# Router logits from the attention output product: a folded gate, and expert weights loaded in another order

## The chip, the cores and the metric

The kernel runs on one core of a Trainium2 chip. The metric is the device time of one execution in microseconds (us); lower is better. A core has five engines with an instruction stream each: TensorE (PE, with its weight loads as PEld), VectorE (DVE), ScalarE (ACT), GpSimd (POOL) and SyncE (SP), which here only issues DMAs. The engines are ordered by semaphores alone.

## The reference

One sequence of T = 1024 tokens of width D = 256 passes a mixer with a gated feed-forward part, a linear mixing layer, causal attention over 8 heads of 64, and a mixture of 8 experts of which each token takes two. Layer normalisations stand between. What the change touches is the seam of the last two:

```python
z = softmax(q k' / 8 + causal mask) v          # 8 heads of 64 columns
x3 = x2 + z @ wo                               # residual, [1024, 256]
h = (x3 - mean(x3)) / sqrt(var(x3) + 1e-5)
logits = h @ gate.T                            # [1024, 8]
top_v, top_i = top_k(softmax(logits), 2)
weights = top_v / sum(top_v)                   # per token
y = x3 + sum over the two: weight * (silu(h @ w1[e]) * (h @ w3[e])) @ w2[e]
```

## The kernel before, in words

The program is written by hand, engine by engine; the order of each stream is the order of the Python loops, and every dependency is a semaphore.

**q, k, v.** 24 blocks (`FILLS`), 12 for each half of the tokens: four of q, four of k, four of v, 512 columns each. TensorE makes a block as 6 products in fp32r (values split in a high and a low part, three part products over two halves of the width, lines 1618 and 1622) into PSUM banks 2 to 7 in turn; it waits only for the block six places back. ScalarE reads k blocks and even blocks, VectorE k blocks and odd blocks. Banks 0 and 1 hold transposed inputs, `hT`, which is the layer-normalised x2.

**Attention.** 8 tiles of 128 tokens (i), 4 pairs of heads each, so 32 steps m = 4i + rel and 6 more that empty the pipeline. In step m TensorE makes `scores(m)`, transposes the probabilities of the heads before (`probs_transposed`, line 1660), and multiplies them with v (`attended(m - 2)`, line 1675, two heads side by side in 64 columns of the array each). Between these, by rel: `reciprocals_transposed(i - 1)` at rel 2, `attention_out(i - 1)` at rel 3 (the product with wo, line 1694, 256 columns into bank 6 or 7). VectorE finds the row maxima before each exponential of ScalarE; at rel 3 it adds the product to x and takes mean and variance (`add_attention`, `route_variance`, to line 1250); GpSimd makes 1/sqrt from it.

**The router of tile t = i - 2** follows a step later. VectorE normalises (line 1254, rel 0), TensorE transposes the rows (1703), ScalarE copies them (803), TensorE multiplies them with the gate (1709, 8 columns), VectorE takes the maximum (1259), ScalarE the exponentials (808), VectorE chooses the two largest at rel 1 (`route_choice`, 1264 to 1272), TensorE counts with two products, a triangle of ones and a full one (`route_counts`, 1718 and 1719), and VectorE makes weights and slot numbers (`route_tail`, `route_slots`, to 1294). GpSimd then scatters each token's row to its two slots of `expert_in` (592). For the last tile all of this stands alone, with `keep_busy` products of no use between, which keep TensorE occupied.

**The seam.** After the last slots VectorE makes a table of expert tiles (1324 to 1341). SyncE loads the first two tiles of slots (436) once table and scatter are done. ScalarE and VectorE split the first expert's weights (849, 1364) when all up matrices are loaded and all of x is stored (`s_out`, line 873).

**Expert weights on SyncE's queue.** w1 and the first four w3 are loaded at the start of attention. Then SyncE stores tiles 0 to 6 of x, each when it is ready (lines 411 to 413), and only then loads w3 of experts 6 and 7, w2 of experts 0 to 4 (when all scores are done), w3 of 4 and 5 (when zT of the last tile is done), w2 of 5 to 7 and the last 64 rows of all w2 (`m_w2t`, a strip of 64 partitions), and stores the last tile of x (432). A w3 matrix is 704 KB, a w2 matrix 640 KB, the strip 512 KB.

**Experts.** 23 tiles of 128 slots. A tile: 2 transposes of its rows (1757), 6 transposes of the activation of the tile before (1777; 704 columns padded with zeros to 768), 18 products up in fp32r (1769), 6 products down in float32, which are 12 records (1789; the sixth has 64 rows of zeros, which lines 586 and 1383 write). TensorE's order in the steady loop:

```python
def body(i, b, first=False):
    pe.wait_ge(s_exT, i + 2)
    expert_x(i + 2, b)
    expert_aT(i, b)
    expert_up(i + 1, 1 - b)
    expert_down(i, b, first)
```

## Time and profile before

| | |
|---|---|
| median of 3 executions | 556.26 us (556.05 to 556.93) |
| the profiled execution | 554.53 us |
| its span, first to last instruction | 552.7 us |
| mean clock granted to TensorE | 0.98 of full speed |
| TensorE / VectorE / ScalarE / GpSimd busy | 508.2 / 356.0 / 278.5 / 184.6 us |
| share of the chain that ended last, TensorE | 76% |
| q, k, v: stretch of the span | 159 to 197 us |
| attention | 197 to 343 us |
| from the last scores' work to the first expert products | 343 to 374 us |
| experts | 374 to 546 us |
| ScalarE's copy of up to 512 columns (line 791), mean | 0.51 us |

The span is what the profiler sees between the first and the last instruction; the execution's own time lies 1.8 us above it. Busy time is no measure of a bound by itself: what an engine waited for, and whether anything waited for it, is in the chain and the waits. A record is one instruction in the trace; a float32 product is two of them.

### The profile page before, as it was taken

The numbers are of one execution on the slowest core, as the hardware profiler recorded it, in microseconds if no ns is written. First come the engines' busy times: TensorE is split into PE (matmuls) and PEld (weight loads), VectorE is DVE, ScalarE is ACT, GpSimd is POOL, SyncE is SP. The second block draws the span as 40 slices with busy tenths as digits, with TensorE's granted clock in tenths as the row PEclk, the third lists the DMA queues.
The fourth block names the chain that finished last, engine by engine and source line by source line (L and its number), as shares of the span: only waits on it lengthen the run. The fifth ranks groups of instructions, "written<-read, shape, count | busy, mean of one in ns | idle before, by whom it ended". The sixth has DMA issues, their size and how long they took to land.

```text
span 552.7 us, 9980 instructions
## 1 busy us (share of the span) xinstructions
PE 508.2 (92%) x3285; PEld 417.9 (76%) x3286; DVE 356.0 (64%) x875; ACT 278.5 (50%) x529; POOL 184.6 (33%) x236
## 2 busy tenths in 40 slices
PE   3988989998989998989999998797999999999994
PEld 1647978887968866667778786676888888888883
DVE  5884879547457335656668675456777777777761
ACT  2585554216123265656555563025666666666651
POOL 3026629984032032422223110310433333333332
PEclk9997999999999999999999999779999999999999
DMA  8999001000010069000000005861112222222211
GB/s 322 406 338 291 2 25 53 1 0 1 2 38 1 0 239 406 34 31 20 11 31 12 20 20 193 311 193 40 23 37 38 38 38 38 38 38 38 29 16 23
DMA packets 25813, 47.47 MB, mean 86 GB/s; under 512 B 2224, under 2 KB 21168, under 8 KB 25392
## 3 DMA queue, kind: packets, MB, share of 16 engines
q1 hardware_dynamic: 21408, 41.76, 21.4%
q0 software_dynamic: 4080, 5.15, 6.3%
q8 instruction: 22, 0.36, 0.3%
q10 hardware_dynamic: 288, 0.08, 0.1%
q14 instruction: 15, 0.12, 0.1%
HBM read 32.01 MB, written 14.98 MB: 85 GB/s over the span
## 4 chain that ended last, share of the span: by engine, by line
PE 76%; DVE 10%; ACT 5%; issue 5%; POOL 1%; DMA 1%; POOLq 0%; SPq 0%; ACTq 0%; DVEq 0%
PE ps L1769 16%; PE ps L1789 11%; PE ps L1562 8%; PE ps L1660 5%; PE ps L1645 4%; PE ps L1675 4%; PE ps L1618 4%; PE ps L1584 4%; PE ps L1777 3%; PE ps L1457 2%; PE ps L1694 2%; PE ps L1622 2%; DVE early L1012 2%; PE ps L1544 1%; ACT work L783 1%
## 5 line engine op out<-in xcount | busy, mean ns | idle before, releaser
L1769 PE MATMUL ps<-split,xsT 128*128 128x512 f32 (+1 forms) x414 | 93.7, 379 | 1.1 <-DVE split L1364 1.0
L1769 PEld LDWEIGHTS ps<-split,xsT 128*128 128x128 f32 x414 | 74.7, 188 | 13.4 <-issue 1.2
L1364 DVE TENSOR_TENSOR split<-early,split 128x1408 fp32r<-128x1408 f32 x46 | 72.8, 1622 | 6.4 <-ACT split L849 6.0
L1789 PE MATMUL ps<-mid,work 128*128 x276 | 63.4, 379 | 0.8 <-ACT work L838 0.8
L849 ACT CAST split<-early 128x1408 fp32r x46 | 62.6, 1365 | 1.1 <-issue 1.1
L615 POOL TENSOR_TENSOR rstd<-mhalf 128x1 f32<-128x1 f32 x23 | 21.7, 942 | 118.7 <-ACT work L845 118.7
L1214 DVE TENSOR_REDUCE nmax<-ps 128x1 f32<-128x128 f32 (+7 forms) x64 | 45.4, 751 | 21.9 <-PE ps L1645 21.7
L1789 PEld LDWEIGHTS ps<-mid,work 128*128 128x128 f32 x276 | 52.0, 190 | 7.0 <-issue 1.0
L1346 DVE TENSOR_TENSOR work<-work,ps 128x704 f32<-128x704 f32 x23 | 20.4, 888 | 42.4 <-PE ps L1769 42.4
L834 ACT ACTIVATE work<-ps 128x704 f32<-128x704 f32 x22 | 16.8, 762 | 48.4 <-PE ps L1769 48.4
L783 ACT ACTIVATE work<-ps,nmax 128x128 f32<-128x128 f32 (+7 forms) x48 | 35.9, 751 | 2.9 <-DVE nmax L1214 2.9
L616 POOL DMA_INDIRECT out<-work,slot_i x23 | 35.8, 1558 | 4.1 <-issue 2.1
L1660 PE MATMUL ps<-cst,work 128*128 128x128 f32 x216 | 31.4, 278 | 1.8 <-DVE work L1220 1.0
L791 ACT COPY work<-ps 128x512 f32<-128x512 f32 (+3 forms) x32 | 16.2, 506 | 32.8 <-PE ps L1660 32.2
L592 POOL DMA_INDIRECT expert_in<-rows,slot_i x16 | 16.3, 1019 | 47.6 <-DVE slot_i L1294 45.1
L1660 PEld LDWEIGHTS ps<-cst,work 128*128 128x128 f32 x216 | 24.2, 141 | 7.1 <-ACT work L783 4.9
L756 ACT ACTIVATE work<-ps 128x512 f32<-128x512 f32 x16 | 9.6, 598 | 34.6 <-PE ps L1562 34.6
L1457 PE MATMUL ps<-rows,early 128*128 128x512 f32 x48 | 23.5, 638 | 1.5 <-ACT rows L645 1.5
L569 POOL CAST q_hi<-mid 128x128 fp32r<-128x128 f32 x32 | 10.0, 311 | 41.7 <-PE ps L1645 41.1
L598 POOL TENSOR_TENSOR rstd<-veps,mhalf 128x1 f32<-128x1 f32 x8 | 4.5, 567 | 56.6 <-DVE veps L1250 56.6
L791 ACT COPY rows<-ps 128x512 f32<-128x512 f32 (+3 forms) x32 | 16.3, 508 | 12.1 <-PE ps L1660 11.6
L1675 PE MATMUL ps<-work,mid 128*64 128x128 f32 x288 | 19.3, 278 | 2.8 <-ACT early L797 2.7
(259 smaller groups left out, 1144.0 us busy)
## 6 DMA issues: line engine op xcount, KB each, us to landing
early<-m_w SPq DMA_DIRECT2D x16, 704.0 KB, 9.1
expert_in<-pad SPq DMA_DIRECT2D x8, 1040.0 KB, 12.3
mid<-m_w SPq DMA_DIRECT2D x8, 640.0 KB, 8.9
work<-expert_in SPq DMA_DIRECT2D x23, 130.0 KB, 2.8
early<-factors SPq DMA_DIRECT2D x1, 2048.0 KB, 11.5
early<-wq SPq DMA_DIRECT2D x1, 2048.0 KB, 15.5
mid<-f_w SPq DMA_DIRECT2D x1, 2048.0 KB, 19.8
rows<-x_in SPq DMA_DIRECT2D x4, 256.0 KB, 3.9
```

Source lines behind the costliest of these rows:

```text
L616: nc.gpsimd.indirect_dma_start(out=out, out_offset=bass.IndirectOffsetOnAxis(ap=dest_now[:, b:b + 1], axis=0), in_=ey[:, b], in_offset=Non ...
L783: nc.scalar.activation(probs[u % 4][:, 0:w], score_row(u), ACT.Exp, bias=nmax[:, u:u + 1], accum_out=psums[:, u:u + 1]).then_inc(s_pr, 1)
L791: nc.scalar.copy(pT[u % 4][:, 0:w], ps[:, pT_banks(u), 0:w]).then_inc(s_pT, 1)
L849: nc.scalar.copy(split_w[0][:, :, w * I:(w + 1) * I], expert_w(e, w)).then_inc(s_whi[w], 1)
L1214: V.tensor_reduce(nmax[:, u:u + 1], score_row(u), AX_X, ALU.max, negate=True).then_inc(s_max, 1)
L1364: V.tensor_tensor(lo, expert_w(e, w), hi.bitcast(F32), ALU.subtract).then_inc(s_wlo[w], 1)
L1457: last = mm(ps[:, 2 + q % 4, :], win_sb[:, k, fb * P:(fb + 1) * P], hT[:, k, g * GW:(g + 1) * GW], start=(k == 0), stop=(k == KD - 1))
L1562: last = mm(ps[:, 2 + 2 * w + q % 2, :], fw13_split[pw][:, w * KD + k, f * P:(f + 1) * P], hT_split[ph][:, k, g * GW:(g + 1) * GW], start= ...
L1660: last = nc.tensor.transpose(ps[:, pT_banks(u) + j // 4, (j % 4) * P:(j % 4 + 1) * P], probs[u % 4][:, j * P:(j + 1) * P], ident)
L1675: last = mm(ps[h * DH:(h + 1) * DH, 6 + i % 2, pair * P:(pair + 1) * P], v_sb[:, j, n * DH:(n + 1) * DH], pT[(2 * m + h) % 4][:, j * P:(j ...
L1769: last = mm(up_flat[:, c0:c1], xsT[px][b][:, k, :], split_w[pw][:, k, c0:c1], start=(k == 0 and px == pw), stop=(k == KD - 1 and px == 1))
L1789: last = mm(ps[:, 6, 0:D], eaT[:, b, c, :], we[:, c, :], start=(c == 0), stop=(c == IB - 1))
```

## The change

The gate (256 x 8) is centred: the mean of each column is subtracted, so that logits of x3 need no subtraction of the row's mean. With a centred gate g, the logits before the factor 1/sqrt(var) are x2 @ g + z @ (wo @ g). `wo @ g` is computed once and put beside wo as 8 more columns (`wo_m`, 264 wide), so that the output product makes it along; x2 @ g is computed from `hT` with the gate as the stationary operand (8 columns), turned to tokens by small products, and multiplied by sqrt(var(x2)) (`base_logit`). The choice is made from these sums right behind the variance; the two weights come from the exponential of the difference of the two largest. Transposes, copy, product with the gate and maximum of the router are gone. The expert loads are interleaved, the last store of x goes to ScalarE's queue, and the last of six transposes and products of an expert tile are cut to the 64 columns and rows that hold data, without the zeros.

```diff
@@ SyncE: loads behind the stores of tiles 0 to 6
-            for e in range(below_k, E):
+            def load_w3(e):
                 pairs_over = -(-(E * KD * I + (e + 1) * KD * I - K_AT) // T)
                 sp.wait_ge(s_sc, (TT - 1) * HEADS + 2 * min(pairs_over, PAIRS))
                 sp.dma_start(ew3[:, e], m_w3[:, e]).then_inc(s_e13, 16)
-            sp.wait_ge(s_sc, TT * HEADS)
+            def load_w2(e):
+                pairs_over = max(0, -(-((e + 1) * IB * D - QB * T) // T))
+                if pairs_over:
+                    sp.wait_ge(s_sc, (TT - 1) * HEADS + 2 * min(pairs_over, PAIRS))
+                sp.dma_start(ew2[:, e, 0:(IB - 1) * D], m_w2[:, e]).then_inc(s_e2, 16)
             below_v = 2 * QB * T // (IB * D)
-            for e in range(below_v):
-                sp.dma_start(ew2[:, e, 0:(IB - 1) * D], m_w2[:, e]).then_inc(s_e2, 16)
+            sp.wait_ge(s_qs, STEPS)
+            for e in range(2):
+                load_w2(e)
+            load_w2(2)
+            load_w3(below_k)
+            load_w2(3)
+            load_w3(below_k + 1)
+            load_w2(4)
             sp.wait_ge(s_zT, TT)
...
-            sp.wait_ge(s_x3, TT)
-            sp.dma_start(out[(TT - 1) * P:T, :], x[:, TT - 1, :]).then_inc(s_out, 16)
@@ GpSimd
-                if i == TT + 1:
-                    pool.wait_ge(s_pv, TT * HEADS // 2)
-                    nc.gpsimd.memset(mid[ILAST:P, :]...., 0.0).then_inc(s_w2pad, 1)
@@ ScalarE
             for q in range(FILLS):
+                if q in (16, 18):
+                    h = (q - 16) // 2
+                    act.wait_ge(s_woTp, h + 1)
+                    nc.scalar.copy(base_T[:, h * GW:(h + 1) * GW], ps[0:E, 1, :])
+                    nc.scalar.copy(woT[:, h, :], ps[:, 0, :]).then_inc(s_woT, 1)
...
-            def routed_feature_major(i):
...
             def logits_exp(i):
-                act.wait_ge(s_lmax, i + 1)
-                nc.scalar.activation(prob_e[:, i, :], ps[:, 6 + i % 2, D:D + E], ACT.Exp, ...)
+                act.wait_ge(s_ldiff, i + 1)
+                nc.scalar.activation(prob_e[:, i, 0:TOP], prob_e[:, i, 0:TOP], ACT.Exp).then_inc(s_lexp, 1)
...
+            act.wait_ge(s_x3, TT)
+            act.dma_start(out[(TT - 1) * P:T, :], x[:, TT - 1, :]).then_inc(s_out, 16)
             act.wait_ge(s_eid, 1)
             act.wait_ge(s_e13, 2 * E * 16)
             act.wait_ge(s_out, (TT + 1) * 16)
@@ VectorE
+            def centre_gate():              # at q == 14
+                dve.wait_ge(s_gsum, 1)
+                link(V.scalar_tensor_tensor(gate_sb, ps[:, 0, 0:E]..., -1.0 / D, gate_sb, ALU.mult, ALU.add))
+                link(V.tensor_copy(gate_r[:, 0], gate_sb))
+                V.tensor_tensor(gate_r[:, 1], gate_sb, gate_r[:, 0].bitcast(F32), ALU.subtract).then_inc(s_gc, 1)
+            def read_gate_fold():           # at q == FILLS - 2
+                link(V.tensor_tensor(spread, veps[:, :], rstd[:, :], ALU.mult))
+                dve.wait_ge(s_fold, 1)
+                V.tensor_copy(wo_m[:, :, D:], ps[:, 1, 0:QB * E]...)
+                V.tensor_tensor(base_logit, ps[:, 1, QB * E:QB * E + TT * E]..., spread..., ALU.mult).then_inc(s_folded, 1)
...
-            def route_max(t):
...
             def route_choice(t):
-                dve.wait_ge(s_lexp, t + 1)
-                link(V.reciprocal(rs[2][:, t:t + 1], rs[1][:, t:t + 1]))
-                link(V.tensor_scalar(prob_e[:, t, :], prob_e[:, t, :], rs[2][:, t:t + 1], None, ALU.mult))
-                link(V.max(top_v[:, t, :], prob_e[:, t, :]))
+                link(V.tensor_tensor(rank_e[:, t, :], ps[:, at, D:D + E], base_logit[:, t, :], ALU.add))
+                link(V.max(top_v[:, t, :], rank_e[:, t, :]))
...
+            def route_difference(t):        # two copies as in route_tail, then
+                V.tensor_scalar(prob_e[:, t, 0:TOP], top_v[:, t, 0:TOP], top_v[:, t, 0:1], rstd[:, t:t + 1],
+                                ALU.subtract, ALU.mult).then_inc(s_ldiff, 1)
+            def route_weights(t):           # waits for s_lexp; sum, reciprocal, product; increments s_slots
...
                 if rel == 3 and 1 <= i <= TT:
                     add_attention(i - 1)
                     route_variance(i - 1)
+                    route_choice(i - 1)
                 if rel == 0 and i >= 2:
-                    route_max(i - 2)
+                    route_normalise(i - 2)
+                    route_difference(i - 2)
+                    route_slots(i - 2)
                 if rel == 1 and i >= 2:
-                    route_tail(i - 2)
-                    route_slots(i - 2)
+                    route_weights(i - 2)
@@ TensorE
+            def gate_sums():                # before block 13
+                pe.wait_ge(s_gate, 32)
+                for k in range(KD):
+                    last = mm(ps[:, 0, 0:E], ones, gate_sb[:, k, :], start=(k == 0), stop=(k == KD - 1))
+                last.then_inc(s_gsum, 1)
+            def fold_inputs(h):             # before blocks 15 and 17; waits for s_wo, s_gc, s_woT
+                for part, (pw, ph) in enumerate(W_PARTS):
+                    for k in range(KD):
+                        mm(ps[0:E, 1, :], gate_r[:, pw, k, :], hT_split[ph][:, k, h * GW:(h + 1) * GW], ...)
+                for c in range(QB):
+                    last = nc.tensor.transpose(ps[:, 0, c * P:(c + 1) * P], wo_m[:, c, h * P:(h + 1) * P], ident)
+                last.then_inc(s_woTp, 1)
+            def gate_folded():              # before block 20; waits for s_woT
+                for c in range(QB):
+                    for k in range(KD):
+                        mm(ps[:, 1, c * E:(c + 1) * E], woT[:, k, c * P:(c + 1) * P], gate_sb[:, k, :], ...)
+                for t in range(TT):
+                    last = mm(ps[:, 1, (QB + t) * E:(QB + t + 1) * E], base_T[:, t * P:(t + 1) * P], ident[0:E, 0:E], ...)
+                last.then_inc(s_fold, 1)
...
             def scores(m):
+                if m == 0:
+                    pe.wait_ge(s_folded, 1)
...
-                    last = mm(ps[:, 6 + i % 2, 0:D], zT[:, c, :], wo_sb[:, c, :], ...)
+                    last = mm(ps[:, 6 + i % 2, 0:D + E], zT[:, c, :], wo_m[:, c, :], ...)
...
-            def route_transposed(i):        # keep_busy(16, 0) for the last tile
...
-            def route_logits(i):
...
             def route_counts(i):
                 if i == TT - 1:
-                    keep_busy(14, 0)
+                    keep_busy(20, 0)
...
-                if rel == 0 and i >= 2:
-                    route_transposed(i - 2)
...
-                if rel == 1 and i >= 2:
+                if rel == 0 and i >= 2:
                     route_counts(i - 2)
                 if 2 <= m <= STEPS + 1:
                     attended(m - 2)
-                if rel == 0 and i >= 2:
-                    route_logits(i - 2)
...
             def expert_x(i, b):
                 if isinstance(i, int) and i == 0:
-                    keep_busy(24, 0)
+                    keep_busy(16, 0)
...
             def expert_aT(i, b):
...
-                    last = nc.tensor.transpose(ps[:, 4 + c // 4, (c % 4) * P:(c % 4 + 1) * P],
-                                               ea[:, b, c * P:(c + 1) * P], ident)
+                    w = P if c < IB - 1 else ILAST
+                    last = nc.tensor.transpose(ps[0:w, 4 + c // 4, (c % 4) * P:(c % 4 + 1) * P],
+                                               ea[:, b, c * P:c * P + w], ident)
...
             def expert_down(i, b, first=False):
...
-                    last = mm(ps[:, 6, 0:D], eaT[:, b, c, :], we[:, c, :], ...)
+                    w = P if c < IB - 1 else ILAST
+                    last = mm(ps[:, 6, 0:D], eaT[0:w, b, c, :], we[0:w, c, :], ...)
...
+            keep_busy(56, 0)
             pe.wait_ge(s_e13, 2 * E * 16)
-            keep_busy(40, 0)
```

## Rows read from the trace of the kernel before

**Rows 1.** Stretches: busy us of PE, PEld, DVE, ACT, POOL; clock; DMA share; GB/s.

```profile
159.00:197.00 38.00, 37.47 (x171) 30.19 (x168) 17.38 (x36) 12.15 (x21) 6.43 (x13) 1.00 0.00 0
197.00:343.40 146.40, 137.45 (x1347) 108.60 (x1345) 95.50 (x270) 85.89 (x219) 37.32 (x75) 1.00 0.24 90
343.40:374.50 31.10, 24.86 (x169) 20.33 (x168) 14.78 (x63) 4.88 (x10) 6.37 (x6) 0.78 0.71 256
```

**Rows 2.** The chain that ended last: start us, us, what; blocks and one expert tile.

```profile
180.32 11.15 PE ps L1618 x48
...
527.14 0.66 PE ps L1777 x6
527.80 3.81 PE ps L1769 x18
531.61 2.59 PE ps L1789 x12
```

**Rows 3.** Timeline of the tail: start us, us, engine, line, operation, idle before.

```profile
341.47 1.97 PE L1675 MATMUL ps<-work,mid 128*64 128x128 f32 x32
...
347.13 3.68 PE L1675 MATMUL ps<-rows,mid 128*64 128x128 f32 x32
...
356.42 0.15 DVE L1250 TENSOR_SCALAR veps<-mv 128x1 f32<-128x1 f32 x1
...
357.27 1.97 DVE L1254 TENSOR_SCALAR rows<-rows,mv,rstd 128x256 f32<-128x256 f32 x1 [0.69 <-POOL rstd L598]
357.29 1.80 POOL L586 MEMSET mid<- 64x2048 f32 x1
...
365.67 0.17 DVE L1294 CAST slot_i<-rs 128x2 uint32<-128x2 f32 x1
...
368.95 0.18 DVE L1341 TENSOR_SCALAR region<-bias_sb 128x24 int32<-128x24 f32 x1
```

**Rows 4.** The chain in the tail: last scatter and first tile's load.

```profile
367.46 2.44 DMA expert_in<-rows,slot_i
...
370.94 2.00 DMA work<-expert_in
```

**Rows 5.** Timeline of TensorE, 312 to 319 us, at changes of the array's form.

```profile
313.32 0.73 PE L1645 MATMUL ps<-k_hi,q_hi 64*128 64x512 f32 x4
...
314.91 0.44 PE L1703 MATMUL ps<-cst,rows 128*128 128x128 f32 x2
315.19 0.93 PE L1660 MATMUL ps<-cst,rows 128*128 128x128 f32 x7
316.05 1.75 PE L1675 MATMUL ps<-work,mid 128*64 128x128 f32 x28
317.73 0.61 PE L1709 MATMUL ps<-gate_sb,rows 128*128 128x8 f32 x4
318.19 1.07 PE L1660 MATMUL ps<-cst,work 128*128 128x128 f32 x8
```

**Rows 6.** Waits of TensorE, 197 to 262 us: total, times, longest.

```profile
PE ps L1718 <- DVE rt L1272: 1.6, 2, 1.0
...
PE ps L1703 <- DVE rows L1254: 0.6, 1, 0.6
```

**Rows 7.** Timeline of SyncE's queue in the tail.

```profile
337.28 0.33 SPq L413 DMA_DIRECT2D out<-rows  x1
...
353.23 0.81 SPq L425 DMA_DIRECT2D early<-m_w  x2
```

**Rows 8.** Stretches of the tail, columns as in rows 1.

```profile
347.00:351.00 4.00, 4.00 (x34) 3.65 (x35) 0.75 (x5) 0.00 (x0) 1.81 (x2) 0.50 1.02 415
351.00:354.00 3.00, 2.95 (x15) 2.22 (x15) 0.69 (x1) 0.59 (x1) 0.18 (x1) 0.72 0.16 58
357.00:359.00 2.00, 0.00 (x0) 0.00 (x0) 1.73 (x1) 0.00 (x0) 1.94 (x2) 1.00 1.01 418
363.00:366.00 3.00, 3.00 (x17) 2.39 (x15) 1.84 (x15) 0.00 (x0) 0.00 (x0) 0.50 1.07 214
```

More of the change, by code:

```diff
@@ L207, in build @@
         base_e = view(dts_t, 0, TT + 1, E)
-        rs_t = sb("rs", 12 * TT)
-        rs = [rs_t[:, i * TT:(i + 1) * TT] for i in range(12)]
-        top_f = view(rs_t, 8 * TT, TT, TOP)
-        slot_f = view(rs_t, 10 * TT, TT, TOP)
+        rs_t = sb("rs", 8 * TT)
+        rs = {n: rs_t[:, i * TT:(i + 1) * TT] for i, n in ((1, 3), (2, 4), (4, 8), (5, 9))}
+        top_f = view(rs_t, 4 * TT, TT, TOP)
+        slot_f = view(rs_t, 6 * TT, TT, TOP)
         top_i_t = sb("top_i", TT * 8, U32); top_i = view(top_i_t, 0, TT, 8)
@@ L219, in build @@
         w_first, w_second = bias_sb[:, 0:24], bias_sb[:, 24:48]
+        base_logit = view(bias_sb, 0, TT, E)
+        spread = rs_t[:, 0:TT]
         dest_now = slot_i_t[:, 0:2]
@@ L282, in build @@
         s_zT, s_ao, s_x3 = sem("zT"), sem("attn_out"), sem("x3")
-        s_rT, s_rTc, s_lg, s_lmax, s_lexp, s_chosen, s_cnt = (sem(n) for n in (
-            "routed_transposed", "routed_T", "logits", "logit_max", "logit_exp", "chosen", "counts"))
+        s_ldiff, s_lexp, s_chosen, s_cnt = (sem(n) for n in (
+            "logit_difference", "logit_exp", "chosen", "counts"))
+        s_gsum, s_gc, s_woTp, s_woT, s_fold, s_folded = (sem(n) for n in (
+            "gate_summed", "gate_centred", "wo_transposed", "wo_T", "gate_folded", "gate_fold_read"))
         s_slots, s_scat, s_table, s_dest = sem("slots"), sem("scattered"), sem("tile_table"), sem("destinations")
@@ L1589, in _ @@
             transposes(PH_ATT, 0)
+            def gate_sums():
[4 more added lines that the diff above has]
+            def fold_inputs(h):
+                pe.wait_ge(s_wo, 16)
+                pe.wait_ge(s_gc, 1)
+                if h:
+                    pe.wait_ge(s_woT, h)
+                for part, (pw, ph) in enumerate(W_PARTS):
+                    for k in range(KD):
+                        mm(ps[0:E, 1, :], gate_r[:, pw, k, :], hT_split[ph][:, k, h * GW:(h + 1) * GW],
+                           start=(part == 0 and k == 0), stop=(part == 2 and k == KD - 1))
+                for c in range(QB):
+                    last = nc.tensor.transpose(ps[:, 0, c * P:(c + 1) * P], wo_m[:, c, h * P:(h + 1) * P], ident)
+                last.then_inc(s_woTp, 1)
+            def gate_folded():
+                pe.wait_ge(s_woT, 2)
+                for c in range(QB):
+                    for k in range(KD):
+                        mm(ps[:, 1, c * E:(c + 1) * E], woT[:, k, c * P:(c + 1) * P], gate_sb[:, k, :],
+                           start=(k == 0), stop=(k == KD - 1))
+                for t in range(TT):
+                    last = mm(ps[:, 1, (QB + t) * E:(QB + t + 1) * E], base_T[:, t * P:(t + 1) * P], ident[0:E, 0:E],
+                              start=True, stop=True)
+                last.then_inc(s_fold, 1)
             pe.wait_ge(s_pwlo, 3)
@@ L1740, in _ @@
                     probs_transposed(2 * m - 1)
-                if rel == 1 and i >= 2:
+                if rel == 0 and i >= 2:
                     route_counts(i - 2)
```

83 lines of the change are left out of this document (35 added, 48 removed).

## The prediction, made before the changed kernel was seen

> **What bounds the kernel now.** I read the page's slices first, then a table of stretches [rows 1]: TensorE is busy 37.5 of 38.0 us while q, k and v are made and 137 of 146 us in attention, but 24.9 of 31.1 us between attention and experts, at a mean clock of 0.78. So what is added to or taken from TensorE counts nearly in full in the first two, and the tail between attention and experts is a chain of waits. The chain in order of time [rows 2] has 48 products of 512 columns back to back, and an expert tile as 6 transposes, 18 products up and 12 records down, each beginning where the last ends: the experts are TensorE's too. The tail by engine [rows 3] shows three losses: the last heads' product with the probabilities (L1675) takes 3.68 us at the low clock after it stood behind the counts of tile 6, where the same work took 1.97 just before; from the last variance (356.57) to the last slots (365.84) lie 9.3 us of router; and in it the normalisation takes 1.97 us beside GpSimd's memset. Then come scatter and load of the first tile [rows 4].
>
> The sum is made against the profiled execution, 554.5 us (span 552.7 and 1.8 around it); the median is 556.3, so I add the difference to the median.
>
> **The fold, new work while q, k, v are made.** Prices: a product of 512 columns 11.15/48 = 0.232, a transpose 0.66/6 = 0.11 [rows 2]; a float32 product with 8 moving columns is two records, four records took 0.46, so 0.115 a record [rows 5]. Gate sums: 4 records, 0.5. Residual part: 12 products of 512 columns, 2.8. Eight transposes of wo, 0.9. Fold: 8 products, 16 records, 1.8; base logits: 8 products, 16 records, 1.8. Together 7.8.
>
> A change of the array's form has a price too. L1675 (128 rows, 64 columns) starts at 316.05, though the seven transposes before it at 0.11 end at 315.96, and it takes 1.68 to L1709 where 14 pairs at 0.11 need 1.54: 0.23 together. L1645 (64 rows) takes 1.59 where 6 pairs at 0.232 need 1.39, and the two records behind it 0.28 for 0.22: 0.26 [rows 5]. Not all of the way in or out is seen in either, so I take 0.3 for in and out. A stationary gate of 8 columns (twice) and base logits of 8 rows (once) make 0.9. **Fold: +8.7**, bounds +6 (small records at half price, as they are short) and +10 (a wait for the centred gate, at most one block of 1.4). The rest is covered: ScalarE's four copies and VectorE's five small instructions lie where both are under half busy [rows 1], six banks ahead; wo lands before; if that cover went, four copies would cost 2 us (0.5 each on the page). Scores wait for the fold, read two blocks (2.8 us) earlier: nothing.
>
> **Attention.** Tiles 0 to 5 lose two transposes and four small records each, 0.22 + 0.46; the output product's 8 more columns on 256 give back 0.05. Six times 0.63 is 3.8. TensorE also stood 1.6 us before the counts and 0.6 before the transposes [rows 6]; the choice now runs right behind the variance, a step ahead of the counts, so I take 1.7 of it. **-5.5**, bounds -7 and -2. Late next is VectorE: its block behind the output product grows by the choice, 1.3 us, ahead of the next maxima. It is 95 of 146 us busy [rows 1], and choice, slots and weights, which stood at one step, are spread over three; the bound of -2 is for the narrow tiles, where ScalarE waits for those maxima.
>
> **The tail.** Tile 6 is chosen before its counts are asked for, so nothing stands before L1675: it starts at 343.4 and ends at 345.4 at the pace of the call before, not at 350.8. With the reciprocals at full clock, zT comes at 347.5 instead of 353.2 and the last variance at 350.9 instead of 356.57 [rows 3, 7]: -5.6. Then choice 1.3; counts 0.7 beside normalisation 0.4 (the memset is gone) and difference 0.5; slots 0.9; weights 0.6, whose exponential on ScalarE lies beside the slots: slots known at 354.6 instead of 365.84, -11.2 in all. Scatter and table follow; the table (3.3 us, to 369.13) stays inside the scatter's 4.1 (to 369.90) [rows 3, 4].
>
> SyncE's queue is moved only in part. The pair-by-pair loads still stand behind the store of tile 6, issued at 337.28 [rows 7], when every score they wait for is done, so nothing starts earlier; only the pause before the second batch goes (58 GB/s from 351 to 354). First batch done at 351; 2 x 704 and 3 x 640 KB at some 416 GB/s, 8.2; scatter and last store among them, 1.0; the 512 KB strip at 214 GB/s, 2.6 [rows 8]: done at 363, landed a little later. The first tile's load, ready at 359.7, lies behind it and lands at 363.8, not 361.7. The tail thus gives 372.9 - 363.8 = 9.1. The last store, now on ScalarE's queue, costs it one issue (0.65) behind its last exponential and lands, even if as late as a scatter's 4.1, hardly after the expert numbers that ScalarE waits for anyway.
>
> The warm-up products (72 x 0.11) end near 360.4, three microseconds before that load. In this tail the clock was at 1.2 GHz in the four and three microseconds that rows 8 show, behind pauses of about 2 us such as the one at 357; if it falls again, the first 6 of 18 products up, 6 x 0.23 at full clock, lose some 1.1 us beyond what their wait hides. **Tail: -8**, bounds -11 (the load doesn't queue) and -6.
>
> **The experts.** Per tile, the last transpose gets 64 stationary columns and the last product 64 rows. Neither moves fewer columns, so I count no gain: L1675's 64-column calls keep the transposes' pace of 0.11 [rows 5]. But that last product stands between full ones. The scores' first head has the very shape (64 rows from partition 0) and ran paired with its neighbour, so the form follows the shape: in and out 0.3, 23 times, and TensorE has no slack: **+6.9**, bounds 0 and +9. For the transpose no row shows a transpose in a narrow form; I take 0, bounds -1.3 (0.055 each if its weights counted) and +6.9. The Trainium skill (TensorEngine Tiling, Key Properties) says that changing the tiling mode drains TensorE, which speaks against this part; the sum is +6.9 by it and 0 without. The same page (Restrictions) rules out transpose mode for float32 under column tiling, which would keep the narrow transpose in the full form.
>
> Sum: +8.7 - 5.5 - 8.0 + 6.9 = +2.1, so 558.4.
>
> **Rivals.** *Both forms change* (in and out 0.3 twice a tile, 46 times): +9.0, 565.3. For it: nothing in the code tells the transpose's shape from another. *No form changes*, since the gaps were the pairs' and not the form's: 7.8 - 5.5 - 8.0 = -5.7, 550.6, faster. For it: the pairs are the only case in the trace; against it, the gaps stand at every change and at none of the 18-to-12 seams. The point between: 3 changes in the fold and 23 in the experts outweigh 5.7 from 0.22 us each. *The loads don't hold the tail and VectorE doesn't hold attention* (-11 and -7): -2.4, 553.9.
>
> **Chances.** Likeliest, only the product changes form: 0.42, by itself 553 to 562. Both: 0.25. None: 0.26. The last: 0.07. A measurement of this kernel tells some 0.2% (1.1 us) from no change. The likeliest case is slower in 6 of 10 of its spread, the same in 2.4, faster in 1.6; the second is slower; the last two are faster but for a tenth. Faster 0.07 + 0.24 + 0.05 = 0.36, same 0.12, slower 0.52. The range 549.5 to 566.5 reaches to both outer cases; what is left out is the far side of each.
>
> **What would show it.** Expert tiles: a period of 7.28 us now (0.66 + 3.81 + 2.59 and two transposes of 0.11) [rows 2]; 7.6 by my sum, 7.9 if both change, 7.3 if none. TensorE from the start of block 13 to the end of block 23: 8.7 longer. The first tile's load landing 9 us nearer to the last scores, directly behind the strip. L1254's last call at 0.4. A clock of 1.2 GHz at the first products up. I am wrong if the period stays at 7.3 us, if TensorE waits for the gate or its copies, or if the loads of the last matrices start before the store of tile 6.

## The result, and the profile after

The changed kernel takes 564.0 us (median; 563.0 to 566.1), the kernel before, run beside it, 556.6 (556.1 to 557.3). The ratio is 1.0154, with a 95% interval of 1.0124 to 1.0183: the change costs 7.4 us between the medians, and 6.9 to 10.2 us by the interval. The profiled execution took 564.9 us, with a span of 563.0.

The starts of the same instructions in both traces divide the difference of the spans (563.0 - 552.7 = 10.3 us):

| stretch, from start to start | before, us | after, us | difference |
|---|---|---|---|
| span's start to the first product for q | 156.5 | 159.4 | +2.9 |
| to the first scores | 40.6 | 51.7 | +11.1 |
| to tile 6's output product | 136.2 | 130.9 | -5.3 |
| to the second expert tile's first product up | 48.6 | 42.3 | -6.3 |
| to the last record of TensorE | 163.3 | 171.2 | +7.9 |

The first line isn't the change's: nothing of that part was edited (the end of this document has what is in it). Without it the traces differ by 7.5 us, about what the medians say.

**The fold.** The page's chain of waits and a table of stretches show it. The timeline of TensorE's products, with one row of VectorE and two of TensorE's weight loads (PEld) put in, kernel after (start us, us busy, engine, line, operation):

```profile
187.24 0.63 PE L1680 MATMUL ps<-hT_lo,qkv_w_hi 128*128 128x512 f32 x2
...
187.52 0.17 DVE L1209 TENSOR_TENSOR gate_r<-gate_sb,gate_r 128x16 fp32r<-128x16 f32 x1
...
187.81 0.58 PEld L1628 LDWEIGHTS ps<-hT_hi,gate_r 128*8 128x8 f32 x4 [0.39 <-issue]
187.84 1.09 PE L1628 MATMUL ps<-hT_hi,gate_r 128*8 128x512 f32 x4
...
189.60 0.72 PE L1680 MATMUL ps<-hT_hi,qkv_w_hi 128*128 128x512 f32 x2
...
192.25 0.78 PEld L1628 LDWEIGHTS ps<-hT_hi,gate_r 128*8 128x8 f32 x4
192.48 1.08 PE L1628 MATMUL ps<-hT_hi,gate_r 128*8 128x512 f32 x4
...
198.50 1.84 PE L1639 MATMUL ps<-gate_sb,early 128*128 128x8 f32 x16
200.27 2.30 PE L1642 MATMUL ps<-cst,early 8*128 8x8 f32 x16
202.50 1.22 PE L1684 MATMUL ps<-qkv_w_hi,hT_hi 128*128 128x512 f32 x2
203.52 1.05 PE L1684 MATMUL ps<-qkv_w_lo,hT_hi 128*128 128x512 f32 x2
```

The first `fold_inputs` adds 1.90 us: two 512-column products after 187.24 end at 187.70 (2 x 0.232), the next block's begin at 189.60. The second adds 1.74 (192.48 to 194.22). The first is longer by a wait of 0.14 us: its weights aren't loaded ahead, as those of the second are (at 192.25, 0.23 us ahead of their product), but at 187.81, just after VectorE has written the last part of the centred gate (187.69). The small records of `gate_folded` take from 198.50 to 202.50, 4.00 us, and the gate sums 0.36. Behind the sums and behind each `fold_inputs` the first pair of products takes 0.56 us to the next pair instead of 0.46, 0.09 more, as it does behind full-width transposes in the kernel before (175.88 to 176.43). That makes 0.36 + 1.90 + 1.74 + 4.00 + 3 x 0.09 = 8.27. Then a pair of products that takes 0.63 us elsewhere takes 1.05, and goes on so until 208.5. The stretches say why (columns as in [rows 1]; the seventh is the granted clock):

```profile
196.00:200.00 4.00, 4.00 (x27) 3.51 (x25) 2.07 (x3) 2.50 (x5) 0.00 (x0) 1.00 0.00 0
200.00:204.00 4.00, 4.00 (x24) 3.67 (x24) 0.01 (x1) 0.00 (x0) 0.00 (x0) 0.71 0.00 0
204.00:208.00 4.00, 4.00 (x11) 3.13 (x10) 0.00 (x0) 0.60 (x1) 0.00 (x0) 0.50 0.00 0
```

TensorE counts as busy in all of it, but its clock fell to 1.2 GHz (0.50 of 2.4) at 201.7, within the last four of the 32 small records. The last 24 products take from 202.50 to 210.93, 8.43 us, where the kernel before has 5.58 (191.31 to 196.89): another 2.85 us. With 8.27 it is the 11.1 of the table. Some 0.3 of the 4.00 us of the small records are the low clock too: the last starts lie 0.22 us apart, the others 0.11.

**The tail.** Chain of waits, kernel after (start us, us, what), the rows that answer to [rows 4]:

```profile
362.28 0.24 DVE rows L1308
...
364.64 5.93 DMA expert_in<-rows,slot_i
...
371.59 2.33 DMA work<-expert_in
```

The timeline beside it, answering to [rows 3, 7] (the bracket is the idle time ahead of an instruction and what ended it):

```profile
346.09 0.33 SPq L419 DMA_DIRECT2D out<-rows  x1
346.46 1.40 SPq L430 DMA_DIRECT2D mid<-m_w  x3
...
359.11 0.15 DVE L1278 TENSOR_SCALAR veps<-mv 128x1 f32<-128x1 f32 x1
...
360.35 0.41 DVE L1282 TENSOR_SCALAR rows<-rows,mv,rstd 128x256 f32<-128x256 f32 x1
361.11 0.36 ACTq L880 DMA_DIRECT2D out<-rows  x1
...
361.81 0.17 DVE L1322 CAST slot_i<-rs 128x2 uint32<-128x2 f32 x1
...
367.45 0.19 ACT L885 COPY veps<-mhalf 128x1 f32<-128x1 f32 x1 [6.15 <-DMA out<-rows]
```

Counted from tile 6's output product (333.33 before, 342.08 after), the last variance comes at 17.2 us instead of 23.2, and slots and weights are written at 20.4 instead of 32.5. Of these 12.1 us only 7.8 reach the first slot rows, for the last scatter takes 5.93 us where it took 2.44. ScalarE stands 6.15 us for the last residual store.

**The experts.** One tile in the chain of waits, kernel after, answering to [rows 2]:

```profile
521.02 0.37 PE ps L1801 x2
521.39 0.65 PE ps L1822 x6
522.05 3.81 PE ps L1813 x18
525.86 2.78 PE ps L1835 x12
528.64 0.37 PE ps L1801 x2
```

The period is 7.62 us (521.02 to 528.64) where it was 7.27. All of it lies in the product down (2.78 for 2.59) and in the two transposes behind it (0.37 for 0.22). The six transposes of L1822, one of them narrow now, take 0.66 as before.

### The profile page after: what moved, and what is told of

Its sections match the earlier page's. It is cut to its first block, busy times and chain, and to the rows that moved or that the text cites. A ratio compares the mean times of both kernels' runs of the same rounds, so it can differ in the third digit from the quotient of the medians.

```text
span 563.0 us, 9974 instructions
## 1 busy us (share of the span) xinstructions
PE 519.5 (92%) x3291; PEld 415.8 (74%) x3292; DVE 353.6 (63%) x872; ACT 277.7 (49%) x517; POOL 181.4 (32%) x235
## 4 chain that ended last, share of the span: by engine, by line
PE 81%; DVE 8%; ACT 4%; issue 2%; DMA 2%; POOL 1%; POOLq 0%; SPq 0%; ACTq 0%; DVEq 0%
PE ps L1813 16%; PE ps L1835 11%; PE ps L1587 8%; PE ps L1709 6%; PE ps L1724 6%; PE ps L1739 4%; PE ps L1680 4%; PE ps L1609 4%; PE ps L1758 3%; PE ps L1822 3%; PE ps L1684 3%; PE ps L1482 2%; DVE early L1022 2%; PE ps L1801 2%; PE ps L1703 1%
## 5 line engine op out<-in xcount | busy, mean ns | idle before, releaser
L1813 PE MATMUL ps<-split,xsT 128*128 128x512 f32 (+1 forms) x414 | 95.1, 383 | 1.0 <-DVE split L1390 1.0
L1813 PEld LDWEIGHTS ps<-split,xsT 128*128 128x128 f32 x414 | 76.1, 191 | 13.3 <-issue 1.2
L1835 PE MATMUL ps<-mid,work 128*128 (+1 forms) x276 | 67.9, 387 | 0.8 <-ACT work L846 0.8
L1835 PEld LDWEIGHTS ps<-mid,work 128*128 128x128 f32 (+1 forms) x276 | 50.1, 189 | 13.4 <-issue 8.7
L1372 DVE TENSOR_TENSOR work<-work,ps 128x704 f32<-128x704 f32 x23 | 20.4, 888 | 47.7 <-PE ps L1813 47.7
L1587 PE MATMUL ps<-hT_hi,ffn_w_hi 128*128 128x512 f32 x64 | 20.7, 404 | 1.4 <-DVE early L1163 1.4
## 6 DMA issues: line engine op xcount, KB each, us to landing
expert_in<-pad SPq DMA_DIRECT2D x8, 1040.0 KB, 12.3
mid<-f_w SPq DMA_DIRECT2D x1, 2048.0 KB, 20.4
```

The source lines that it names most:

```text
L1587: last = mm(ps[:, 2 + 2 * w + q % 2, :], fw13_split[pw][:, w * KD + k, f * P:(f + 1) * P], hT_split[ph][:, k, g * GW:(g + 1) * GW], start= ...
L1813: last = mm(up_flat[:, c0:c1], xsT[px][b][:, k, :], split_w[pw][:, k, c0:c1], start=(k == 0 and px == pw), stop=(k == KD - 1 and px == 1))
L1835: last = mm(ps[:, 6, 0:D], eaT[0:w, b, c, :], we[0:w, c, :], start=(c == 0), stop=(c == IB - 1))
```

## The experiments

### The form of the experts' last product

`e1_full_width`, the kernel after with these lines as before, and both zero fills in their old places:

```diff
-                    w = P if c < IB - 1 else ILAST
-                    last = nc.tensor.transpose(ps[0:w, ...], ea[:, b, c * P:c * P + w], ident)
+                    last = nc.tensor.transpose(ps[:, ...], ea[:, b, c * P:(c + 1) * P], ident)
...
-                    last = mm(ps[:, 6, 0:D], eaT[0:w, b, c, :], we[0:w, c, :], ...)
+                    last = mm(ps[:, 6, 0:D], eaT[:, b, c, :], we[:, c, :], ...)
```

> The kernel after, but the experts' last transpose and last product go back to full width (128 columns of activation, 128 rows of weight), with both zero fills put back where the kernel before had them. Nothing else differs from the kernel after. Theory (the change of form is what the experts lost): the period of a slot tile goes from 7.62 back to 7.28 us, the entry of the last product from 0.32 to 0.22 us, and the time falls by 22 x 0.35 = 7.7 us, less up to 0.3 us for the zero fill on GpSimd beside the last tile's work: near 556.5 us, a ratio to the kernel before near 1.000 to 1.002. Rival (the period comes from something else the change altered, such as where the weights lie or when copies run): the period stays at 7.6 and the time within 1 us of 564. A second rival (the tail's fills cost more than that): the period falls but the time falls by 5 us or less.

Measured: 556.7 us, ratio 1.0003 (0.9980 to 1.0026). Its chain:

```profile
521.81 0.22 PE ps L1807 x2
...
526.51 2.59 PE ps L1839 x12
529.10 0.22 PE ps L1807 x2
```

The period is 7.29 again (521.81 to 529.10), and 7.4 us are gone. The rest of the change, router and loads, is together worth nothing against the kernel before, as it stands in this run. The zero fill on GpSimd costs more here than the 0.3 us expected: the last tile's normalisation takes 1.58 us beside it, 0.41 in the kernel after, and from tile 6's output product to the second expert tile's first product up it is 43.6 us instead of 42.3.

`e2_narrow_product` puts back only the full transposes and the fill of their padding columns.

> The kernel after with only the last transpose of the expert activations back at full width (and its zero fill of the padding columns on VectorE); the last product keeps its 64 rows. Theory from the gaps between single records of the kernel after: the product's form takes 0.105 on entry, 0.09 on leaving and 0.055 behind it, 0.25 in all, and the transpose 0.10; so the period falls from 7.62 to 7.52 us and the time by 2 us, to near 562. Rival A (the transpose costs all of it, the product's form nothing): period 7.28, time near 556.5. Rival B (the transpose costs nothing): period 7.62, time as after.

Measured: 564.7 us, ratio 1.0156 (1.0123 to 1.0188), the kernel after's own. Its chain:

```profile
527.98 0.37 PE ps L1803 x2
528.35 0.66 PE ps L1823 x6
...
532.83 2.78 PE ps L1836 x12
535.61 0.37 PE ps L1803 x2
```

The period stays at 7.63, so rival B holds: the narrow transpose costs nothing, and 0.35 us a tile is the product's form alone.

`e10_before_narrow` does that one thing to the kernel before:

```diff
-                    last = mm(ps[:, 6, 0:D], eaT[:, b, c, :], we[:, c, :], start=(c == 0), stop=(c == IB - 1))
+                    w = P if c < IB - 1 else ILAST
+                    last = mm(ps[:, 6, 0:D], eaT[0:w, b, c, :], we[0:w, c, :], start=(c == 0), stop=(c == IB - 1))
```

> The kernel before with one edit: the experts' last product takes 64 rows instead of 128; transposes, zero fills and all else stay. Theory (each tile pays 0.35 us at the two changes of form): the period of a slot tile goes from 7.27 to 7.62 us, 22 times, and the time up by 7.7 us, to near 563.5, a ratio of 1.0135 to 1.0145. Rival (the form costs only beside the other parts of the change): period 7.27 and no change.

Measured: 564.0 us beside 556.8, ratio 1.0130 (1.0102 to 1.0158). TensorE's timeline:

```profile
520.72 0.44 PE L1757 MATMUL ps<-cst,work 128*128 128x128 f32 x2
...
525.45 2.95 PE L1790 MATMUL ps<-mid,work 128*128 x12
528.33 0.44 PE L1757 MATMUL ps<-cst,work 128*128 128x128 f32 x2
```

From 520.72 to 528.33 it is 7.61. That one edited product costs 7.3 us between the medians.

### The clock behind the fold

`e7_after_again` is the kernel after, unchanged.

> The kernel after once more, unchanged. It tells how much of the 2.5 us by which the two kernels with another fold placement and with earlier loads came out ahead belongs to the chip's clock from one execution to the next. Theory: 563 to 565 us, with the fall of the clock to 1.2 GHz behind the fold's small products again (3.4 or 6.8 us of it); the fall at 78 us for 3.4 us may come or not, and moves everything behind it by some 2 to 3 us. Rival (the fall behind the fold was an accident of one execution): no fall at 200 us, and near 561 us.

Measured: 564.2 us, ratio 1.0152 (1.0120 to 1.0184). In its trace too the clock is at 1.2 GHz for 6.8 us behind the fold, and the first product for q to the first scores takes 51.72 us, as in the first profile.

`e3_fold_spread`:

```diff
-                if q == 20:
-                    gate_folded()
+                if q in (19, 20):
+                    gate_folded(range(2 * (q - 19), 2 * (q - 18)), ())
+                if q in (21, 22):
+                    gate_folded((), range(GT * (q - 21), GT * (q - 20)))
...
-                if q == FILLS - 2:
+                if q == FILLS - 1:
                     read_gate_fold()
```

> The kernel after with the same 24 small products of the fold (16 for the gate folded into the output weights, 8 for the base logits), but spread over four places: eight ahead of block 19, eight ahead of block 20, four ahead of block 21 and four ahead of block 22, instead of all ahead of block 20. VectorE reads them ahead of its copy of block 23 instead of 22. Same work, same forms. Theory (the fold's 4 us of products with 8 moving columns in one piece let TensorE's clock fall to 1.2 GHz for 6.8 us, in which the values' blocks ran at 0.42 instead of 0.23 us a product): the granted clock stays at 2.4 GHz there, the stretch from the first projection to the first scores shortens by 3 to 4 us, and so does the time, to 560 to 561; the extra entries and exits of the form take up to 0.6 back. Rival A (the clock falls all the same, since the small products are as many): no change, or slower by the 0.6. Rival B (the later read of VectorE now holds the first scores): a wait of TensorE for it shows ahead of the first scores and gives back up to 1.5 us.

Measured: 561.8 us, ratio 1.0109 (1.0078 to 1.0141). Its stretches behind the small products:

```profile
200.00:204.00 4.00, 4.00 (x22) 3.23 (x22) 1.08 (x4) 0.00 (x0) 0.00 (x0) 1.00 0.00 0
204.00:208.00 4.00, 3.98 (x29) 2.65 (x29) 1.75 (x6) 2.77 (x7) 1.26 (x4) 1.00 0.18 28
```

The clock stays at 2.4 GHz, and the stretch takes 49.5 us, 2.2 less than in the kernel after. That is less than the 3 to 4 expected. The low clock cost 2.85 us and some 0.3 in the small records, so the spreading costs about 1.0 itself: TensorE stands idle for 0.23 us (0.39 later from start to start) ahead of the first eight records, for ScalarE's second copy of wo, which has less time now, and three more groups of small records mean three more ways in and out.

### The weight stream and the tail

`e4_loads_ahead`:

```diff
-            for t in range(TT - 1):
+            for t in range(TT - 2):
                 sp.wait_ge(s_x3, t + 1)
...
             load_w2(4)
+            sp.wait_ge(s_x3, TT - 1)
+            sp.dma_start(out[(TT - 2) * P:(TT - 1) * P, :], x[:, TT - 2, :]).then_inc(s_out, 16)
             sp.wait_ge(s_zT, TT)
```

> The kernel after with the seven expert loads that only wait for pairs of tile 7's scores issued ahead of the store of tile 6's rows on SyncE's queue, not behind it. In the kernel after that store waits until 346.1 us, while the last scores are done at 342.2 and the first three pairs of them by 335.9. Theory (the weight stream of some 8 MB, at its rate near 420 GB/s, ends the tail: it holds the last scatter, 5.93 us instead of 2.44, and the residual store for which ScalarE waits 6.15 us): the loads begin 4 to 10 us earlier, the last scatter takes 2.5 to 4 us, ScalarE's wait shortens to 2 to 4 us, the first expert tile's rows land 2 to 3.5 us earlier, and the time falls by 2 to 3.5 us, to near 561. Rival A (the second part of the stream, which waits for tile 7's attention output at 355.9, is long enough alone to reach past the scatter): the scatter stays over 5 us and the time within 0.7 us of 564. Rival B (ScalarE and VectorE read the first expert's weights later than the rows land): rows land earlier but the steady experts start as before.

Measured: 561.5 us, ratio 1.0099 (1.0063 to 1.0134). The time fell, but the stretches from the trace say not by this:

```profile
345.00:350.00 5.00, 5.00 (x77) 4.74 (x77) 2.96 (x15) 1.21 (x3) 1.04 (x1) 1.00 0.02 3
350.00:355.00 5.00, 4.47 (x32) 3.50 (x30) 2.47 (x10) 0.15 (x1) 1.53 (x2) 1.00 0.67 219
355.00:360.00 5.00, 4.64 (x43) 4.07 (x42) 4.42 (x24) 0.20 (x1) 1.36 (x2) 1.00 1.01 418
```

The first part of the stream is over by 345, then hardly anything moves (3 GB/s) until the second part is released at 350.9; that part alone reaches past the scatter. ScalarE still waits 6.31 us for the store, and from tile 7's output product (350.93) to the first slot rows' transpose (368.71) it is 17.8 us, where it was 18.1. Rival A holds for the tail. What else the time fell by (2.5 us to the kernel after in the medians, where rival A had allowed 0.7) lies, in the profiled executions, ahead of attention: the first product for q starts 3.4 us earlier, and the clock is low for 3.4 us behind the fold instead of 6.8, which makes that stretch 1.6 us shorter. Nothing in the edit accounts for either, so whether the earlier loads are worth more than 0.3 us is left open. The run shows one thing more: the stream's last piece, the strip, lands at 364.9, 1.7 us before the first slot rows are asked for, and still they come only 0.3 us nearer. So the slow scatter is enough to hold them.

`e5_w2_behind` moves the issue of the last 2.4 MB:

```diff
-            sp.wait_ge(s_pv, TT * HEADS // 2)
-            for e in range(below_v, E):
-                sp.dma_start(ew2[:, e, 0:(IB - 1) * D], m_w2[:, e]).then_inc(s_e2, 16)
-            sp.dma_start(mid[0:ILAST, :] ... m_w2t).then_inc(s_e2, 16)
...
             for b in range(2):
                 load_slots(b, b)
+            sp.wait_ge(s_pv, TT * HEADS // 2)
+            for e in range(below_v, E):
+                sp.dma_start(ew2[:, e, 0:(IB - 1) * D], m_w2[:, e]).then_inc(s_e2, 16)
+            sp.dma_start(mid[0:ILAST, :] ... m_w2t).then_inc(s_e2, 16)
```

> The kernel after, with the last part of the weight stream (the second expert weights 5 to 7 and the 64-row strip, 2.4 MB, not used before the experts' first last product at 388 us) issued on SyncE's queue behind the first two loads of slot rows, not ahead of the last scatter. Theory (the weight stream holds the last scatter and the last residual store): the last scatter lands 2.4 to 3 us after its issue instead of 5.93, ScalarE's wait for the store falls from 6.15 to about 2.5 us, the first slot rows land 3 to 4 us nearer behind the output product of tile 7 (18.1 us in the kernel after), and the time falls by 2.5 to 4 us. Rival A (a scatter of 128 rows behind another one takes its 6 us by itself now, as it did when the stream was moved ahead by the earlier loads): the distance from output product to first slot rows stays at 17.5 to 18.1 us and the time within 0.8 us. Rival B (the moved 2.4 MB now lie across the loads of the next slot rows, or the first last product waits for them): the rows land earlier, but the steady experts begin no earlier.

Measured: 562.1 us, ratio 1.0103 (1.0074 to 1.0132). Its chain:

```profile
362.70 2.45 DMA expert_in<-rows,slot_i
...
369.12 0.67 SPq L455
...
371.34 8.23 DMA work<-expert_in
```

Theory and rival B are both seen. The scatter takes 2.45 us again, ScalarE waits 4.85 instead of 6.15, and the first rows come 14.3 us behind tile 7's output product (353.96 to 368.22), 3.8 nearer. But the third tile's rows now need 8.23 us behind the moved weights on the same queue, so the second tile's products up begin only 1.9 us nearer. TensorE waits there for two things: for these rows, landed at 379.6, and for the strip, landed at 379.3, since its program waits for all of the second expert weights (`s_e2`) ahead of the third tile's transposes and not only ahead of the first tile's last product, as the expectation had it. In this trace 1.4 of the 1.9 us are lost again at once: the second tile's products up take 5.4 us instead of 4.0, for the clock is at 1.2 GHz from 380.4 for 3.4 us. The medians fall by 2.1; what the rest of that is, the trace doesn't show.

`e6_store_back` puts the last residual store on SyncE's queue again:

```diff
                          m_w2t).then_inc(s_e2, 16)
+            sp.wait_ge(s_x3, TT)
+            sp.dma_start(out[(TT - 1) * P:T, :], x[:, TT - 1, :]).then_inc(s_out, 16)
...
-            act.wait_ge(s_x3, TT)
-            act.dma_start(out[(TT - 1) * P:T, :], x[:, TT - 1, :]).then_inc(s_out, 16)
```

> The kernel after with the store of tile 7's residual rows back where the kernel before had it: on SyncE's queue behind the strip of the weights, not on ScalarE's queue. Theory (on SyncE's queue it lands with the end of the weight stream or behind it, and ScalarE's first weight copy waits for it): ScalarE's first weight copy starts 1 to 2.5 us later than in the kernel after, VectorE's remainder behind it, but the slot rows land only at 373.9, so at most 1 us of the first experts goes: the time is 0 to 1 us longer. Rival (the ScalarE queue's store takes DMA engines from the last scatter, whose 5.93 us stand on the chain that ends last): the scatter shortens by 1 us or more and the time falls by as much.

Measured: 566.8 us, ratio 1.0185 (1.0152 to 1.0218), 2.5 us above the repeat of the kernel after measured beside it. Timeline:

```profile
358.87 1.23 SPq L450 DMA_DIRECT2D out<-rows  x1
...
363.50 0.96 POOL L606 DMA_INDIRECT expert_in<-rows,slot_i  x1 [0.30 <-issue]
...
370.58 26.01 SPq L454 DMA_DIRECT2D work<-expert_in  x6
...
372.57 0.19 ACT L885 COPY veps<-mhalf 128x1 f32<-128x1 f32 x1 [12.40 <-DMA out<-rows]
```

ScalarE waits 12.4 us, so its weight copies begin 18.7 us behind tile 7's output product (354.75 to 373.44) where the repeat has 12.3: 6.4 us later, not the 1 to 2.5 of the expectation, and now they end last. The scatter isn't shorter: from its issue at 363.50 to the load's at 370.58 is 7.1 us, in the repeat 7.05. From tile 7's output product to the second tile's first product up it is 31.4 us, in the repeat 28.7. So the move of the store, which the prediction counted at nothing, is worth some 2.5 us with the stream as it lies.

### Put together

`e8_all_mended` has full width, the spread fold, the earlier loads and the end of the stream behind the first slot rows; the zero fill of the strip stands on GpSimd behind the last scatter.

> The kernel after with four edits together: the experts' last product and transposes at full width (zero fill of the weight strip on GpSimd behind the last scatter), the fold's small products spread over four blocks, the seven loads ahead of the store of tile 6, and the end of the weight stream behind the first slot rows. Theory: 564 less 7.6 for the form, 2 to 3.5 for the clock, 0 to 1 for the earlier loads and 2.5 to 4 for the freed scatter: 548 to 552 us, a ratio to the kernel before of 0.985 to 0.993, faster than both. Rival (the scatter isn't freed, the rest holds): 552 to 555. Second rival (the router fold costs at its place what it saves in attention and the tail, whatever the placement): 556, no faster than the kernel before.

Measured: 553.7 us, ratio 0.9957 (0.9938 to 0.9975), above the range expected. The timeline shows what the theory had left out, though the run with the moved weights had shown it too:

```profile
370.78 28.06 SPq L449 DMA_DIRECT2D work<-expert_in  x5
...
378.92 0.29 PEld L1810 LDWEIGHTS ps<-cst,work 128*128 128x128 f32 x2 [5.61 <-DMA mid<-m_w2t]
```

TensorE waits 5.6 us. The strip, which the profile names, lands at 378.6 and the third tile's rows at 378.8, and TensorE's program waits for both here. `e9_stream_split` divides what was moved:

```diff
+            for e in range(below_v, E - 1):
+                sp.dma_start(ew2[:, e, 0:(IB - 1) * D], m_w2[:, e]).then_inc(s_e2, 16)
...
             for b in range(2):
                 load_slots(b, b)
+            sp.dma_start(ew2[:, E - 1, 0:(IB - 1) * D], m_w2[:, E - 1]).then_inc(s_e2, 16)
+            for b in range(2):
+                sp.wait_ge(s_ext, b + 1)
+                sp.wait_ge(s_dest, b + 1)
+                load_slots(b + 2, b)
+                if b == 0:
+                    sp.dma_start(mid[0:ILAST, :] ... m_w2t).then_inc(s_e2, 16)
+            with sp.Fori(1, LAST // 2 - 1) as j:
```

> The kernel with four edits, but the end of the weight stream is divided: second expert weights 5 and 6 ahead of the last scatter again (behind the first weights 6 and 7, 2.7 MB from 353.0 us at 420 GB/s, landed by about 359.5, ahead of the scatter's issue at 360.4), the weights 7 directly behind the first two slot loads, and the 64-row strip behind the third. Theory (in the kernel with four edits the third tile's rows took 8.04 us to land behind 2.4 MB on the same queue, and TensorE waited 5.3 us for them): the scatter still takes 2.5 to 3 us, the third load lands in 3 to 4 us, the distance from the output product of tile 7 to the first steady product of the experts falls from 27.5 to 24 to 25 us, and the time from 553.7 to near 550.5. Rival A (the scatter meets the stream again): the first rows land 1.5 us or more later, and the time stays within 1 us. Rival B (the first last product now waits for the strip): a wait of TensorE ahead of it, and the gain is under 1 us.

Measured: 550.1 us, ratio 0.9885 (0.9853 to 0.9917). The timeline:

```profile
362.46 0.96 POOL L613 DMA_INDIRECT expert_in<-rows,slot_i  x1 [0.30 <-issue]
...
371.74 1.09 SPq L465 DMA_DIRECT2D mid<-m_w2t  x1
...
377.86 0.20 PEld L1817 LDWEIGHTS ps<-cst,work 128*128 128x128 f32 x2 [2.58 <-DMA mid<-m_w2t]
```

The scatter stays short and TensorE's wait falls from 5.6 to 2.6 us. These 2.6 are the expectation's rival B: the third tile's rows land at 373.7, the strip only at 377.8. A kernel that waits for the strip just ahead of its first product down wasn't run. From tile 7's output product (353.72) to the second tile's first product up (378.71) it is 25.0 us, against 28.5 in the kernel after. This version beats the kernel before by 6.7 us in the medians (550.1 to 556.8) and the changed one by about 14.

## Why the prediction was right or wrong

The time, 564.0, lies in the range, on the side that had the larger chance, 5.6 us above the number given. That it lies in the range is in part luck: the fold took 11.1 us, outside its bounds of 6 to 10, and the range went up to 566.5 for the sake of a rival (both forms change) that the runs refute.

- **The fold's own work was near**: 8.3 for 8.7. The small records took 4.0 for 3.6 without the change of form, with some 0.3 of low clock in it. The change of form was over-rated: 0.3 was taken for each of the two pieces with 8 stationary columns, and the second shows none (the 0.09 behind it stands behind full-width transposes too). The 0.14 ahead of the first is a wait for the centred gate, one of the signs of being wrong that the prediction names, though far smaller than the block of 1.4 us that its bound allowed. Nothing waits for the copies here, but the first small records of the spread fold do.
- **The fold's clock was the first failed step.** "Together 7.8" plus three changes of form priced the small records by their own durations, at full clock. What stands behind them wasn't asked: 2.85 us in the blocks that follow. The spread fold shows that it is the small records in one piece that do it. The prediction had looked for falls of the clock only where TensorE stood idle; here it was busy all the time.
- **Attention was right**: -5.3 for -5.5. The wait for the choice (1.6 us in [rows 6]) is gone, and VectorE doesn't hold the narrow tiles.
- **The tail was over-rated by 1.7**: -6.3 for -8, still inside its bounds of -11 to -6. Variance (-6.0 for -5.6) and slots (-12.1 for -11.2) came as worked out, and the zero fill's victim, the normalisation, took 0.41. The loads began right behind tile 6's store, as said. The failed step is scatter and load of the first tile. It left the scatter at its old pace, and the stream slows it, 5.93 us for 2.44, as the run that moves the weights shows. It also let the stream end 29.7 us behind tile 6's output product (363 to 333.3): the load does land with the strip, as said (373.9 and 373.7), but that is 31.7 us behind. The first batch of the stream was taken to last 13.7 us (337.3 to 351) and lasts 15.9 (346.5 to 362.3). Either holds the first rows at about the same time; the run with the earlier loads shows that the scatter is enough by itself. The ramp of the first experts costs 1.5 more (8.9 to 10.4 us from the first transpose to the second tile's products up) where 1.1 was taken for the clock, which did fall to 1.2 GHz there.
- **"Hardly after the expert numbers that ScalarE waits for anyway" was wrong** for the last store: it lands 6 us after its issue and ScalarE waits for it. The move is still worth making, since the store in its old place costs some 2.5 us more.
- **The experts were right in mechanism and a little small**: +7.9 for +6.9. In and out of the 64-row form is 0.35 us a tile, not 0.3; 22 periods (the prediction counted 23) make 7.7; taking the form out of the kernel after and putting it alone into the kernel before moved the time by 7.4 and 7.3. The form follows the shape of the product and not the scores' pairing, and the transpose changes nothing. So both outer rivals fall, the one with 46 changes of form and the one with none.

The Trainium skill (TensorEngine Tiling, Key Properties) says that a change of tiling mode drains the array. The runs agree for the product with 64 rows, at 0.35 us. The Trainium skill (the same page, Restrictions) rules out transpose mode for float32 under column tiling; that the transpose to 64 columns pays nothing agrees with it. But the products with 8 stationary columns pay nothing at their seams either, so no run here separates the page's reason from another.

The sum with what was measured is 8.27 + 2.85 - 5.28 - 6.26 + 7.91 = +7.5. The 5.4 us that it stands above the +2.1 of the prediction are the clock (2.9), the tail (1.7), the experts (1.0) and attention (0.2), less 0.4 in the fold.

What stays open: how much the earlier loads bring by themselves, whether the fold could cost less, and what a later wait for the strip would bring. With it spread it adds 8.9 us, more than attention's 5.3, and pays only together with the shorter tail.

## What to carry to other kernels

Cutting padding from one product in a chain of full ones saves nothing where the moving columns stay the same, and costs two changes of the array's form each time: 22 tiles at 0.35 us are 7.7, and the medians moved by 7.3 and 7.4. Small products put between large ones are priced with what runs behind them, for the clock can fall though TensorE is never idle; spreading them kept it up. When a chain gets shorter beside a long weight stream, look at which transfers now meet it, and order the queue by when each piece is waited for: 4.3 of the 12.1 us that the router won did not reach the first rows, and 3.8 came back when the last weights were moved behind the scatter. Take that wait from the program, not from the first use: here the strip was waited for some five to seven microseconds before the products that read it.

## What the runs showed of the hardware that was not expected

TensorE's clock fell at the end of 32 records with 8 columns each, while the engine counted as 4.00 of 4.00 us busy; it was at 1.2 GHz for 6.8 us in five of the seven profiles with the fold in one piece and for 3.4 in the other two (the full-width kernel and the one with the earlier loads), and not at all behind the fold in the three with it spread.

The clock also differs between executions in a part that no kernel here changes. The kernel after, its first layers:

```profile
80.00:84.00 4.00, 4.00 (x16) 3.40 (x15) 3.63 (x9) 1.79 (x3) 0.54 (x1) 0.72 0.06 10
```

and the kernel before in the same stretch:

```profile
80.00:84.00 4.00, 4.00 (x19) 3.18 (x18) 3.79 (x14) 0.60 (x1) 1.22 (x2) 1.00 0.56 150
```

A fall of 3.4 or 6.8 us near 78 us is in eight of the twelve profiles, the kernel before with its one narrow product among them, and not in the kernel before itself. What it costs is seen between two writes of ScalarE: 17.0 us in the kernel before, which has no fall there (70.05 to 87.06), 17.9 in the kernel after with a fall of 3.4 us (72.19 to 90.05), and 19.4 in `e9_stream_split` with the one fall of 6.8 us (70.54 to 89.96). So it is some 0.8 of the 2.9 us in the table's first line. The other 2.1 are there by 51 us, and begin with the second load of the input (from the chain of waits, kernel before and kernel after):

```profile
1.22 3.48 DMA rows<-x_in
1.21 4.33 DMA rows<-x_in
```

Why that load took 0.85 us longer is open. So two profiles of this kernel are compared stretch by stretch, not by their spans.

A move between queues can matter more than the transfer's size: the same 128 KB store took 6.2 us on ScalarE's queue and 13.5 us behind the weights on SyncE's.
